# Filler products, job halves in gaps and moved gathers around the second top-k search of an attention and expert kernel

## The chip, the cores and the metric

The kernel runs on one core of a Trainium2 chip. The metric is the device time in microseconds of one execution. The core has a matrix engine (TensorE, PE in the rows), a vector engine (VectorE, DVE), an activation engine (ScalarE, ACT), a general engine (GpSimd, POOL) that also issues indirect DMAs, and a queue engine (SyncE, SP) for the other DMAs. Each runs its own instructions strictly in the order written, and they wait for one another through semaphores.

## The reference

Two sequences of 1024 tokens with 128 channels go through differential attention with 8 heads, a layer norm, an expert layer of 8 experts with top-256 tokens per expert, and a second layer norm:

```python
    x = L0_attn_X
    x = _layernorm(x + _L0_attn_ref(x, ...), axis=-1)
    x = _layernorm(x + _L0_ffn_ref(x, L0_ffn_gate_w, L0_ffn_w1, L0_ffn_w2), axis=-1)

    # the expert layer, B = 2, T = 1024, E = 8, cap = 256
        scores = jnp.einsum('BTC,CE->BTE', x, gate_w)
        probs = jax.nn.softmax(scores, axis=-1)
        top_p, top_idx = jax.lax.top_k(jnp.transpose(probs, (0, 2, 1)), cap)
        xin = jnp.take_along_axis(x[:, None, :, :], top_idx[..., None], axis=2)
        h = jax.nn.gelu(jnp.einsum('BElC,ECH->BElH', xin, w1), approximate=False)
        y = jnp.einsum('BElH,EHC->BElC', h, w2) * top_p[..., None]
        out = jnp.zeros((B, T, C), x.dtype).at[b_idx, top_idx].add(y)
```

## The kernel before, in words

Every precise matrix product is three products of float32r parts (high by high, high by low, low by high; function `three`). So each operand is rounded by one engine (the high part) and subtracted by another (the low part).

The attention takes 128 steps (16 pairs of sequence and head, 8 query tiles each). In the main loop each engine does its share of several tiles at different stages, in an order written out by hand. The expert layer of sequence 0 is prepared inside that loop: gate, search, indices, first gathers.

Behind the loop come the last outputs (`output(116)` to `output(127)`), and then what the change touches, for sequence 1 (called batch 1):

1. GpSimd computes the factors of the last outputs in groups of four (`norm_end`: a sum L632 and a power L634) once ScalarE has squared them (L814). It gathers rows for the experts of batch 0 (`gather_rows`, L651) between these groups. VectorE adds the outputs (`add_out`, L1071) with those factors.
2. TensorE transposes x1 (`x1_transposes`, L1617), VectorE copies it, TensorE multiplies it with the gate (L1628), and VectorE and ScalarE form the softmax. It is replicated, transposed again (`row_transposes`, L1642) and copied: the left half by VectorE, the right half by ScalarE (`rows_copy`, L833). ScalarE also loads the table of the Gelu here (`tick`, L962).
3. The search finds the 256th largest probability of each expert in 8 levels. In each VectorE counts (`level_count`, L1242), TensorE adds up the votes (`votes`, L1651), VectorE takes the step (`level_step`, L1258). Between them stand halves of the expert jobs of batch 0, by the table `LAST`, which names the last half done ahead of each level's vote.
4. Behind the search TensorE does small products (`limit`, `offset`, `tokens`, `counts`), VectorE the steps between them, and the indices of batch 1 come out (L1332).
5. There are 16 expert jobs (8 experts of each batch). Job q has two halves n = 2q and 2q + 1. For each job TensorE transposes the gathered rows in (`rows_in`, L1832), does `up` and, three halves later, `down`, and transposes out (`rows_out`, L1865); ScalarE rounds and does the Gelus (L881, L883); VectorE forms low parts (L1339, L1367). Jobs of batch 0 are scattered by GpSimd with an adding DMA (`scatter`, L668) into two tables in memory. Jobs of batch 1 are scaled on VectorE (L1354, L1359) and added up on TensorE with one-hot matrices (`mix`, L1876).
6. At the end SyncE loads both tables of batch 0 back (`x2_in`), VectorE adds them (`add_parts`, L1132), and TensorE turns the mixed sums of batch 1 (L1889), which VectorE adds (`add_mixed`, L1141). Then come the means (L1100), the squares on ScalarE (`ln_squares`, L768) and VectorE (`late_squares`, L1150), the variances (L1114), the powers on GpSimd (`ln_pows`, L563), and the scaling (L982, L1123) and the stores.

In the names of buffers, `xk_hi` and `xk_lo` hold expert rows here, `at_hi` and `at_lo` the results of the Gelu, `prob`, `attn` and `raw_a` are reused as storage, and `ring_a`, `ring_b`, `t_ps`, `x_ps`, `u_ps`, `o_ps` are the accumulation buffers of TensorE.

## Time and profile before

| | us |
|---|---|
| three runs, median (lowest, highest) | 909.9 (909.48, 911.5) |
| the profiled execution, its own time | 909.54 |
| span of that profile | 907.8 |
| TensorE busy / weight loads | 866.8 / 729.4 |
| ScalarE, VectorE, GpSimd busy | 748.7, 692.2, 639.6 |
| mean granted TensorE clock | 0.986 |

The span is the time from the first to the last instruction. Positions in the profile are microseconds from the span's start. A granted clock of 1.0 is TensorE at full speed and 0.50 at half. Busy times of TensorE are modelled from pipelined products, so a product's own duration is longer than the distance from its start to the start of the next.

### The profile page before, as it was taken

The numbers are of one execution on the slowest core, as the hardware profiler recorded it, in microseconds if no ns is written. First come the engines' busy times: TensorE is split into PE (matmuls) and PEld (weight loads), VectorE is DVE, ScalarE is ACT, GpSimd is POOL, SyncE is SP. The second block draws the span as 40 slices with busy tenths as digits, with TensorE's granted clock in tenths as the row PEclk, the third lists the DMA queues.
The fourth block names the chain that finished last, engine by engine and source line by source line (L and its number), as shares of the span: only waits on it lengthen the run. The fifth ranks groups of instructions, "written<-read, shape, count | busy, mean of one in ns | idle before, by whom it ended". The sixth has DMA issues, their size and how long they took to land.

```text
span 907.8 us, 14912 instructions
## 1 busy us (share of the span) xinstructions
PE 866.8 (95%) x4598; PEld 729.4 (80%) x4598; DVE 692.2 (76%) x1163; ACT 748.7 (82%) x1449; POOL 639.6 (70%) x1031
## 2 busy tenths in 40 slices
PE   6889999999999999999999999999999999877995
PEld 5668888888888888888888888888888888776984
DVE  5777777777777777777777768778898787578675
ACT  3888898888888888888889888988888889665754
POOL 1777767667776777676778866667776677769782
PEclk9999999999999999999999999999999999979898
DMA  6010010101010101001010020000000001332233
GB/s 180 13 43 16 30 31 1 59 1 58 1 59 1 47 13 36 12 19 30 1 30 1 19 58 18 15 18 16 7 24 1 19 1 44 114 82 48 50 37 99
DMA packets 41663, 30.66 MB, mean 34 GB/s; under 512 B 5825, under 2 KB 39649, under 8 KB 41585
## 3 DMA queue, kind: packets, MB, share of 16 engines
q1 hardware_dynamic: 38256, 26.44, 9.7%
q0 software_dynamic: 3328, 3.28, 2.5%
q8 instruction: 37, 0.61, 0.3%
q14 instruction: 42, 0.34, 0.1%
HBM read 20.14 MB, written 9.57 MB: 33 GB/s over the span
## 4 chain that ended last, share of the span: by engine, by line
PE 81%; POOL 6%; DVE 5%; issue 4%; ACT 2%; DMA 1%; POOLq 0%; SPq 0%; DVEq 0%; ACTq 0%
PE t_ps L1580 11%; PE ring_a L1541 6%; PE ring_a L1543 6%; PE ring_a L1542 6%; PE ring_b L1541 6%; PE ring_b L1543 6%; PE u_ps L1541 6%; PE ring_b L1542 6%; PE u_ps L1543 6%; PE u_ps L1542 6%; PE o_ps L1541 2%; PE o_ps L1542 2%; PE o_ps L1543 2%; PE x_ps L1541 2%; PE x_ps L1543 2%
## 5 line engine op out<-in xcount | busy, mean ns | idle before, releaser
L640 POOL TENSOR_TENSOR attn<-prob 128x1024 f32<-128x1024 f32 x128 | 307.4, 2402 | 173.5 <-ACT prob L799 161.8
L1056 DVE TENSOR_TENSOR at_lo<-t_ps,at_hi 128x512 fp32r<-128x512 f32 x253 | 174.1, 688 | 100.7 <-ACT at_hi L782 100.4
L1049 DVE TENSOR_REDUCE negmax<-ring_a 128x1 f32<-128x1024 f32 x128 | 156.7, 1224 | 58.6 <-PE ring_a L1543 55.7
L782 ACT ACTIVATE at_hi<-t_ps 128x512 fp32r<-128x512 f32 x253 | 151.6, 599 | 39.8 <-PE t_ps L1580 38.7
L1049 DVE TENSOR_REDUCE negmax<-ring_b 128x1 f32<-128x1024 f32 x128 | 156.2, 1220 | 2.7 <-PE ring_b L1543 1.1
L1580 PE MATMUL t_ps<-ident,attn 128*128 128x128 f32 x1012 | 152.1, 272 | 4.3 <-DVE at_lo L1056 4.1
L799 ACT ACTIVATE prob<-prob,coef 128x1024 f32<-128x1024 f32 x128 | 147.6, 1153 | 5.7 <-POOL coef L604 5.6
L1580 PEld LDWEIGHTS t_ps<-ident,attn 128*128 128x128 f32 x1012 | 124.4, 140 | 30.0 <-DVE at_lo L1056 9.4
L793 ACT ACTIVATE prob<-ring_a,negmax 128x1024 f32<-128x1024 f32 x128 | 143.1, 1118 | 4.6 <-DVE negmax L1049 4.1
L793 ACT ACTIVATE prob<-ring_b,negmax 128x1024 f32<-128x1024 f32 x128 | 142.4, 1112 | 0.6 <-DVE negmax L1049 0.5
L1541 PE MATMUL ring_b<-xt_hi,q_hi 128*128 128x512 f32 x256 | 112.0, 438 | 0.0
L1541 PE MATMUL ring_a<-xt_hi,q_hi 128*128 128x512 f32 x256 | 107.3, 419 | 0.5 <-ACT prob L793 0.4
L1543 PE MATMUL ring_a<-xt_hi,q_lo 128*128 128x512 f32 x256 | 101.3, 396 | 0.0
L1543 PE MATMUL ring_b<-xt_hi,q_lo 128*128 128x512 f32 x256 | 101.3, 396 | 0.0
L1542 PE MATMUL ring_a<-xt_lo,q_hi 128*128 128x512 f32 x256 | 100.5, 393 | 0.0
L1542 PE MATMUL ring_b<-xt_lo,q_hi 128*128 128x512 f32 x256 | 100.4, 392 | 0.0
L1541 PE MATMUL u_ps<-at_hi,xk_hi 128*128 128x512 f32 x248 | 97.8, 394 | 2.0 <-DVE u_lo L1062 2.0
L1543 PE MATMUL u_ps<-at_hi,xk_lo 128*128 128x512 f32 x248 | 97.3, 392 | 0.0
L1542 PE MATMUL u_ps<-at_lo,xk_hi 128*128 128x512 f32 x248 | 96.6, 390 | 0.0
L596 POOL TENSOR_TENSOR rs<-psum,neg_one 128x1 f32<-128x1 f32 x128 | 70.5, 551 | 14.7 <-ACT prob L793 14.5
L814 ACT ACTIVATE osq<-o_ps 128x256 f32<-128x256 f32 x117 | 44.9, 384 | 38.3 <-PE o_ps L1543 38.2
L624 POOL TENSOR_TENSOR fac<-var_o,neg_half 128x1 f32<-128x1 f32 x116 | 63.7, 549 | 16.5
(450 smaller groups left out, 1792.6 us busy)
## 6 DMA issues: line engine op xcount, KB each, us to landing
attn<-in_L_ffn_w SPq DMA_DIRECT2D x12, 256.0 KB, 3.3
ww_dram<-ww_hi SPq DMA_DIRECT2D x8, 192.0 KB, 2.5
ww_dram<-ww_lo SPq DMA_DIRECT2D x8, 192.0 KB, 2.9
ww_hi<-ww_dram SPq DMA_DIRECT2D x8, 192.0 KB, 2.4
ww_lo<-ww_dram SPq DMA_DIRECT2D x8, 192.0 KB, 2.5
wq_s<-in_L_attn_Wq SPq DMA_DIRECT2D x8, 128.0 KB, 2.7
wk_s<-in_L_attn_Wk SPq DMA_DIRECT2D x8, 128.0 KB, 3.1
xres<-in_L_attn_X SPq DMA_DIRECT2D x2, 512.0 KB, 6.3
```

The lines of the kernel that those rows point to most:

```text
L596: pool.tensor_tensor(rs2[:, par:par + 1], psum2[:, par:par + 1], neg_one[:, :], ALU.pow).then_inc(rs2_ready, 1)
L624: pool.tensor_tensor(fac[:, par:par + 1], var_o[:, par:par + 1], neg_half[:, 0:1], ALU.pow).then_inc(fac_ready, 1)
L640: pool.tensor_tensor(attn[:, t % AB, :], prob[:, t % 2, 1, :], prob[:, t % 2, 0, :], ALU.add).then_inc(attn_ready, 1)
L782: act.activation(at_hi[:, g % 2, half * GT:(half + 1) * GT, c], t_bank(t, half)[:, :].rearrange("p (k q) -> p k q", q=P), ACT.Copy).then_i ...
L793: act.activation(prob[:, par, m, :], ring[m][:, :], ACT.Exp, bias=negmax[:, par, m:m + 1], accum_out=sums).then_inc(prob_ready, 1)
L799: act.activation(prob[:, par, 1, :], prob[:, par, 1, :], ACT.Copy, scale=coef[:, par:par + 1]).then_inc(scaled_ready, 1)
L1049: dve.tensor_reduce(negmax[:, par, m:m + 1], ring[m][:, :], axis=AX.X, op=ALU.max, negate=True).then_inc(negmax_ready, 1)
L1056: dve.tensor_tensor(at_lo[:, g % 2, k, c], t_bank(t, half)[:, :].rearrange("p (k q) -> p k q", q=P), at_hi[:, g % 2, k, c].bitcast(F32), A ...
L1541: pe.matmul(dst, a_hi, b_hi, start=start, stop=False)
L1542: pe.matmul(dst, a_hi, b_lo, start=False, stop=False)
L1543: return pe.matmul(dst, a_lo, b_hi, start=False, stop=stop)
L1580: last_t = pe.transpose(t_bank(t, half)[:, k * P:(k + 1) * P], attn[:, t % AB, kk * P:(kk + 1) * P], ident[:, :])
```

## The change

In the four programs of the engines that take part:

- TensorE: 26 products whose results nobody reads (`idle_work`, 384 columns each) stand around the x1 transposes and the row transposes of batch 1. Halves of jobs 4 to 6 move between the small products behind the search. The `down` halves and the `mix` products of the last jobs stand in another order.
- GpSimd: seven of the fourteen gathers for batch 0 behind the loop stand earlier.
- ScalarE: the copy of the right half of the rows stands ahead of the Gelu's table load and `tick`. All eight squares of batch 0's norm stand ahead of the copies of the mixed sums.
- VectorE: both groups of `add_parts` stand ahead of job 15's rows, and both variances ahead of `add_mixed`.

```diff
@@ gpsimd
             norm(115)
-            for n in range(2, 7):
+            for n in range(2, 8):
                 gather_rows(n // CT, n % CT)
             norm_end(END)
-            for n in range(7, 9):
+            for n in range(8, 11):
                 gather_rows(n // CT, n % CT)
             norm_end(END + GT)
             norm_end(END + 2 * GT)
             ln_pows(1, 0)
             ln_pows(1, 1)
-            gather_rows(4, 1)
+            for n in range(11, 13):
+                gather_rows(n // CT, n % CT)
             pool.wait_ge(ln_done, 4)
             for e in range(2, E):
                 if e >= RAWS:
                     w_round(e)
                 w_lower(e)
                 if e % 2 == 1:
-                    for k in range(CT):
-                        gather_rows(5 + (e - 3) // 2, k)
+                    n = 13 + (e - 3) // 2
+                    gather_rows(n // CT, n % CT)
@@ scalar
             gate_rep(1)
+            rows_copy(1, 1)
             act.activation(tick[:, 0:1], eps_c[:, :], ACT.Gelu)
-            rows_copy(1, 1)
...
-            for c in range(GT):
+            for c in range(QT):
                 ln_squares(2, c)
             for h in range(2):
                 act.wait_ge(mixed, h + 1)
                 act.activation(sum_t[:, h * NC:(h + 1) * NC], mix_ps[h][:, :], ACT.Copy).then_inc(sum_copied, 1)
-            for c in range(GT, QT):
-                ln_squares(2, c)
@@ vector
             ffn(2 * JOBS + 1)
-            add_parts(0)
-            ln_means(2, 0)
+            for h in range(2):
+                add_parts(h)
+                ln_means(2, h)
             ffn(2 * JOBS + 3)
-            add_parts(1)
-            ln_means(2, 1)
             ln_vars(2, 0)
+            ln_vars(2, 1)
             for h in range(2):
                 add_mixed(h)
                 ln_means(3, h)
-            ln_vars(2, 1)
             late_squares()
@@ tensor
+            def idle_work(dst, count):
+
+                for _ in range(count):
+                    pe.matmul(dst, ww_hi[:, 1, 0:P], ww_hi[:, 1, 0:WWN], start=True, stop=True)
+
+            pe.wait_ge(y_added, 122)
+            idle_work(ring[0][:, 0:WWN], 4)
             x1_transposes(1, 0)
+            idle_work(ring[0][:, 0:WWN], 6)
             rows_in(0)
+            idle_work(ring[0][:, 0:WWN], 2)
             x1_transposes(1, 1)
             gate(1, range(GT))
             gate(1, range(GT, QT))
             ffn(0)
             ffn(1)
+            idle_work(quarter[2][:, 0:WWN], 6)
             row_transposes(1, 0)
             row_transposes(1, 1)
+            idle_work(quarter[2][:, 0:WWN], 8)
...
             last = LAST[LEVELS - 1]
+            down(last - 2)
             limit(1)
+            rows_in((last + 1) // 2 + 1)
+            up(last + 1)
             offset(1)
+            up(last + 2)
             tokens(1)
             counts(1, 0)
             counts(1, 1)
-            for n in range(last + 1, 2 * JOBS + 2):
+            rows_out((last + 2) // 2 - 2)
+            down(last - 1)
+            for n in range(last + 3, 2 * JOBS):
                 ffn(n)
                 if n >= 2 * E + 6 and n % 2 == 0:
                     mix(n // 2 - 3)
-            ffn(2 * JOBS + 2)
-            mix(JOBS - 2, [0])
-            ffn(2 * JOBS + 3)
-            mix(JOBS - 2, [1])
+            down(2 * JOBS - 3)
+            down(2 * JOBS - 2)
+            mix(JOBS - 3, [0])
+            rows_out(JOBS - 2)
+            down(2 * JOBS - 1)
+            mix(JOBS - 3, [1])
+            rows_out(JOBS - 1)
+            mix(JOBS - 2)
             mix(JOBS - 1)
```

What stands in a row on GpSimd behind the loop, from the last factor of the loop to the first low part of a weight (L651 is a gather, L632 and L634 are `norm_end`, L563 `ln_pows`), before:

```order
L651 DMA xg<-xg_dram,idx 128x136 x5
L632 TENSOR_TENSOR var_e<-ssq_e,es 128x4
L634 TENSOR_TENSOR fac_e<-var_e,neg_half 128x4
L651 DMA xg<-xg_dram,idx 128x136 x2
L632 TENSOR_TENSOR var_e<-ssq_e,es 128x4
L634 TENSOR_TENSOR fac_e<-var_e,neg_half 128x4
```

and in the change:

```order
L651 DMA xg<-xg_dram,idx 128x136 x6
L632 TENSOR_TENSOR var_e<-ssq_e,es 128x4
L634 TENSOR_TENSOR fac_e<-var_e,neg_half 128x4
L651 DMA xg<-xg_dram,idx 128x136 x3
L632 TENSOR_TENSOR var_e<-ssq_e,es 128x4
L634 TENSOR_TENSOR fac_e<-var_e,neg_half 128x4
```

One gather more stands ahead of the factors of outputs 116 to 119, and two more ahead of those of outputs 120 to 123.

On ScalarE, behind the softmax of the gate of batch 1 (the second row is the replication, the copy of rows reads `x_ps`, and `xk_hi` begins job 1), before:

```order
L822 ACTIVATE pr<-pr 128x64
L827 ACTIVATE prob<-pr 128x512
L962 ACT_TABLE_LOAD
L962 ACTIVATE tick<-eps_c 128x1
L833 ACTIVATE prob<-x_ps 128x512
L851 ACTIVATE xk_hi<-o_ps 128x256
L881 ACTIVATE at_hi<-ring_a 128x512
```

and in the change:

```order
L823 ACTIVATE pr<-pr 128x64
L828 ACTIVATE prob<-pr 128x512
L834 ACTIVATE prob<-x_ps 128x512
L964 ACT_TABLE_LOAD
L964 ACTIVATE tick<-eps_c 128x1
L852 ACTIVATE xk_hi<-o_ps 128x256
L882 ACTIVATE at_hi<-ring_a 128x512
```

The table load has moved behind the copy, which itself waits for the row transposes.

On VectorE at the end, from the first `add_parts` on (L1132 before, L1131 in the change; `u_hi` and `u_lo` are job 15's rows, `stat` a variance), before:

```order
L1132 SCALAR_TENSOR_TENSOR xres,rsum<-xres,attn 128x128 x4
L1100 TENSOR_SCALAR nmean<-rsum 128x4
L1354 TENSOR_TENSOR u_hi<-ring_b,prob 128x256
L1359 SCALAR_TENSOR_TENSOR u_lo<-ring_b,prob,u_hi 128x128 x2
L1132 SCALAR_TENSOR_TENSOR xres,rsum<-xres,attn 128x128 x4
L1100 TENSOR_SCALAR nmean<-rsum 128x4
L1114 TENSOR_SCALAR stat<-stat 128x4
L1141 SCALAR_TENSOR_TENSOR xres,rsum<-u_ps,xres 128x128 x4
```

and in the change:

```order
L1131 SCALAR_TENSOR_TENSOR xres,rsum<-xres,attn 128x128 x4
L1099 TENSOR_SCALAR nmean<-rsum 128x4
L1131 SCALAR_TENSOR_TENSOR xres,rsum<-xres,attn 128x128 x4
L1099 TENSOR_SCALAR nmean<-rsum 128x4
L1353 TENSOR_TENSOR u_hi<-ring_b,prob 128x256
L1358 SCALAR_TENSOR_TENSOR u_lo<-ring_b,prob,u_hi 128x128 x2
L1113 TENSOR_SCALAR stat<-stat 128x4 x2
L1140 SCALAR_TENSOR_TENSOR xres,rsum<-u_ps,xres 128x128 x4
```

Job 15's rows have moved behind the second group of adds, and both variances stand together behind them.

## Rows read from the trace of the kernel before

**Rows 1.** Busy time by stretch: us, engines busy (instructions), granted clock, DMA share, GB/s.
```profile
796.40:800.20 3.80, 1.62 (x13) 1.17 (x12) 3.19 (x19) 2.87 (x13) 1.45 (x3) 1.00 0.07 19
...
800.60:803.80 3.20, 3.20 (x16) 3.20 (x17) 2.01 (x8) 1.93 (x8) 2.21 (x3) 0.50 0.02 5
...
807.30:810.50 3.20, 0.91 (x7) 0.51 (x5) 2.74 (x6) 2.77 (x7) 3.12 (x3) 1.00 0.09 26
...
834.40:837.80 3.40, 0.99 (x6) 0.82 (x6) 3.04 (x16) 0.51 (x2) 3.04 (x2) 1.00 0.32 42
...
842.00:893.24 51.24, 49.22 (x347) 45.60 (x345) 34.64 (x73) 29.47 (x68) 37.25 (x29) 0.97 0.36 60
```

**Rows 2.** Timeline of GpSimd, 787 to 803: start, duration, what, idle before it.
```profile
787.38 1.37 POOL L651 DMA_INDIRECT xg<-xg_dram,idx  x1 [0.30 <-issue]
789.70 0.20 POOL L632 TENSOR_TENSOR var_e<-ssq_e,es 128x4 f32<-128x4 f32 x1 [0.95 <-ACT osq L814]
...
792.61 1.06 POOL L651 DMA_INDIRECT xg<-xg_dram,idx  x1 [0.30 <-issue]
794.56 0.20 POOL L632 TENSOR_TENSOR var_e<-ssq_e,es 128x4 f32<-128x4 f32 x1 [0.89 <-ACT osq L814]
...
801.77 1.04 POOL L563 TENSOR_TENSOR stat<-stat,neg_half 128x4 f32<-128x4 f32 x1 [0.81 <-DVE stat L1114]
```

**Rows 3.** Timeline of VectorE, 795 to 811.
```profile
795.91 0.35 DVE L1071 SCALAR_TENSOR_TENSOR xres<-ring_a,fac_e,xres 128x128 f32<-128x128 f32 x1 [1.93 <-POOL fac_e L634]
...
803.40 0.23 DVE L1197 TENSOR_TENSOR pr<-t_ps,stat 128x64 f32<-128x64 f32 x1 [0.68 <-PE t_ps L1628]
...
810.74 0.15 DVE L1258 TENSOR_SCALAR step<-x_ps 128x1 int32<-128x1 f32 x1
```

**Rows 4.** Timeline of ScalarE, 805 to 810.
```profile
805.86 1.28 ACT L962 ACT_TABLE_LOAD   x1
807.15 0.20 ACT L962 ACTIVATE tick<-eps_c 128x1 f32<-128x1 f32 x1
807.78 0.60 ACT L833 ACTIVATE prob<-x_ps 128x512 f32<-128x512 f32 x1 [0.43 <-PE x_ps L1642]
...
809.02 0.62 ACT L883 ACTIVATE ring_a<-ring_a 128x512 f32<-128x512 f32 x1
```

**Rows 5.** Timeline of TensorE: two output products, first rows, gate products, job 8.
```profile
795.90 0.33 PE L1542 MATMUL o_ps<-ww_lo,u_hi 128*128 128x384 f32 x1
796.07 0.34 PE L1543 MATMUL o_ps<-ww_hi,u_lo 128*128 128x384 f32 x1
...
798.93 0.41 PE L1832 MATMUL u_ps<-ident,xg 128*128 128x128 f32 x2 [1.14 <-DVE xres L1071]
...
800.15 3.21 PE L1628 MATMUL t_ps<-gate_c,prob 128*128 128x8 f32 x16
...
851.05 0.39 PE L1541 MATMUL ring_a<-xk_hi,q_hi 128*128 128x256 f32 x1 [1.07 <-DVE xk_lo L1339]
```

**Rows 6.** Timeline of VectorE, search and indices, 819 to 842.
```profile
819.62 0.69 DVE L1367 TENSOR_TENSOR at_lo<-ring_a,at_hi 128x512 fp32r<-128x512 f32 x1 [0.32 <-ACT ring_a L883]
...
840.28 0.69 DVE L1329 TENSOR_REDUCE red<-prob 128x8 f32<-128x512 bf16 x1 [1.33 <-ACT prob L837]
841.08 0.17 DVE L1332 SCALAR_TENSOR_TENSOR idx<-red,tok_c 128x8 int32<-128x8 f32 x1
```

**Rows 7.** Timeline of GpSimd: the first gather of batch 1.
```profile
842.15 1.10 POOL L651 DMA_INDIRECT prob<-xg_dram,idx  x1 [0.62 <-DVE idx L1332]
```

**Rows 8.** The chain of waits, its last 15 us: start, duration, what.
```profile
892.78 0.95 DVE xres L1132 x8
...
894.95 1.19 PE t_ps L1876 x4
...
902.24 1.12 DVE xres L1123 x4
```

**Rows 9.** Timeline of VectorE, 900 to 902.
```profile
900.84 0.29 DVE L1114 TENSOR_SCALAR stat<-stat 128x4 f32<-128x4 f32 x2
```

## The prediction

> **What bounds the kernel now.** I read the slices of the page first (TensorE is near full until the last tenth), then the busy time by stretch, then the chain of waits and the timelines behind the last attention output, since the change touches nothing earlier. Four chains follow one another there.
>
> First, from the last outputs to the second search: VectorE waits 1.93 us for GpSimd's factors, and GpSimd had itself waited 0.95 and 0.89 us for ScalarE's sums behind each of its two groups of gathers [rows 2, 3]. Then the 16 gate products take 3.21 us, because the granted clock has fallen to 0.50, the 1.2 GHz level, and VectorE waits the last 0.68 us for them [rows 1, 3, 5]. The reader should see that before the fall TensorE had done little but transposes. Second, the search: VectorE's, almost without a gap; the one that a slow TensorE causes is 0.32 us [rows 6]. Third, from the first index on, GpSimd: its first gather for batch 1 starts at 842.15 [rows 7], and 16 gathers and 12 scatters run one behind another until the last scatter has landed and is loaded back, at 892.78 [rows 8]. Fourth, the end: sums, job 15's rows, last products, norms [rows 8, 9]. TensorE is busy 49.22 of the 51.24 us of the third part, but it waited at its end for VectorE, which stood behind that load.
>
> **The change, step by step.** The sum is made against the profiled execution, 909.54 us (span 907.8 and 1.74 around it); it lies 0.36 under the median of 909.9.
>
> GpSimd's gathers. The last gather of the first group runs 787.38 to 788.75; a sixth adds an issue of 0.30 and some 1.05, so the sum behind it starts at 790.15 and not 789.70: 0.45 later. In the second group a third gather ends at 792.61 + 1.06 + 0.30 + 1.05 + 0.45 = 795.47, and the sum behind it starts at 795.5 and not 794.56: 0.94 later [rows 2]. The wait of 0.89 us that was to hide it had already been eaten by the first 0.45. VectorE waits for exactly this [rows 3], and behind its adds stand the x1 transposes, the means, ScalarE's squares and GpSimd's last power, 801.77 to 802.81 [rows 2], which moves to 803.75. Bounds: 0 if a gather overlaps the wait after all, 1.35 if neither wait hides anything. I take 0.94, since the rows give both ends.
>
> Filler products. 12 products of 384 columns stand around the x1 transposes, 6 ahead of the row transposes and 8 behind them. At full clock one costs 0.17 us (795.90 to 796.07 [rows 5]): 0.7 for the first four, which wait for VectorE's second add and end about when its fourth does, so they delay by 0 to 0.2; 1.0 for six, under a wait like the 1.14 us ahead of the first expert rows [rows 5]; 1.4 for eight, in a stretch where TensorE was busy only 0.91 of 3.20 us [rows 1]. I expect them to hold the clock. The gate products then end before GpSimd's power, and VectorE's gate step starts at 803.80 (power at 803.75) and not 803.40: +0.40 in all, the slow clock's 0.68 being repaid. The Trainium skill, TensorE: Matmul & The Clock Gate, "PE-mode transpose", says that a transpose does not count as busy for the clock; the fall behind 1.62 us of mostly transposes agrees [rows 1], and by that rule the stretch with only transposes and gate products in it remains a place where the clock may fall (the slower rival below).
>
> Row transposes and table load. ScalarE's replication ended at 805.86; with +0.40, 806.26. The two sets of row transposes behind it took until 807.75 at half clock and should be done by 807.2, so the copy of rows starts at 807.2 and not 807.78 [rows 4]. But the table load, 1.28 us plus 0.20 for the tick [rows 4], used to run under these transposes and now stands behind the copy: 807.2 + 0.60 + 1.28 + 0.20 = 809.3, then rounding and the two Gelus as before, the second at 810.05 and not 809.02. VectorE counts the first level earlier, but in its order the first job's low part stands ahead of the level's step, and it needs that Gelu, ending at 810.67. One operation of 0.60 us later the step comes at 811.28 and not 810.74 [rows 3]: +0.54. Bounds: -0.4 (no gather delay) to +0.9 (transposes no faster). The Trainium skill, ScalarE: Activation LUTs, "What ACT_TABLE_LOAD costs", puts a switch at 2.66 us, 1.38 of it a drain. Here the tick starts 1.29 us after the load; by the page the sum would be 1.38 higher.
>
> Search and indices. The search is VectorE's order, which does not change. It gets back the 0.32 us [rows 6]. Behind it TensorE now does job halves (down 9, up 12, up 13) between the small products. Each half is 6 products of 256 columns, an estimated 0.12 each by the 0.17 of 384 columns, some 0.8 us. In the stretch TensorE is idle 2.4 of 3.4 us [rows 1], in three gaps, so VectorE's small steps there don't wait for them. Their inputs are ready, since GpSimd, relieved of two gathers ahead of its last weights (an added one stands in its wait for x1), is some 2 us ahead. The stretch fills up, the clock stays, and the two products that made VectorE wait 1.33 us [rows 6] save some 0.24. The first index comes at 0.54 - 0.32 - 0.24 = -0.02.
>
> GpSimd's queue. Its first gather started 0.90 us after the index operation had ended (841.25 to 842.15), having waited 0.62 [rows 6, 7], because a scatter had only just ended. With three gathers gone from between its wait for x1 and that point it will sit and wait. I take 0.4 for that start, so -0.5 (bounds -0.7 and 0). What follows is the same 28 transfers: the load lands 0.5 earlier.
>
> TensorE in between. Job 8's first product waited 1.07 us for its rows' low parts [rows 5]; with the work ahead of it done earlier TensorE could be an estimated 1 to 2.4 us ahead from there (half the slow stretch before it is the upper end). None of it reaches the end: VectorE forms job 15's rows only after the load.
>
> The end. Before, the load released one group of adds (0.95), then job 15's rows, then the last products at 894.95 [rows 8]. Now both groups of adds stand ahead of job 15: +1.03, with TensorE, the turned sums and both later chains behind it. Repaid: GpSimd's power for the second half leaves the queue ahead of the batch 1 power. Before, the last scaling came at 902.24, behind two powers. Now it hangs on VectorE's four late squares, whose variance step is at 900.84 [rows 9], plus GpSimd's 0.2 to start and 1.1: 902.1 less the 0.13 of the step that has moved away, so the queue's gain is 0.17 to 0.27. I take +0.86 for the end; it would be -1 only if the load came ahead of job 15's rows.
>
> Sum: 0.54 - 0.32 - 0.24 - 0.5 + 0.86 = +0.34, so 909.9 us. All of it is below the 1.8 us (0.2%) that a measurement of this kernel tells from no change.
>
> **Rivals.**
> Faster, 908.1: the two queue costs don't arise. The gathers fit under GpSimd's waits (-0.94), and the load comes before TensorE reaches job 15's rows (-0.86). For it: waits of 0.95 and 0.89 stand where gathers are added. Against it: a gather with its issue is 1.35, longer than either, and GpSimd's 28 transfers leave no room to land earlier.
> Faster still, 907.1: TensorE's own chain sets the end, as its 49.22 of 51.24 busy us suggest, and up to 2.4 us reach it. Against: in the chain of waits it is the DMA and VectorE that come last [rows 8].
> Slower, 913.5: the clock falls in spite of the fillers, in the stretch from the last filler of the first dozen over the x1 transposes and the gate products to the next job half; nearly 3 us of it hold no other product. Then the 16 gate products again take 3.21, two job halves some 3.0 (12 products of twice 0.12 and their rows' transposes), the six fillers 6 x 0.33 = 2.0, and the row transposes 1.5, so the copy of rows starts at about 810.8 and not 807.2. That is +3.6 on the forecast. It decides once TensorE ends behind VectorE's replication by more than the 0.3 us it has in hand. For it: the fall with 1.62 of 3.80 us of mostly transposes.
> Slower by the drain, 911.3: if the moved table load costs 1.38 more than its row.
> It doesn't do what it says, 910.4: the fillers hold the clock first but it falls in the search or behind it as before, and 0.32 and 0.24 are not gained.
>
> **How the numbers follow.** Forecast 0.51, rival 908.1 0.17, rival 907.1 0.06, rival 913.5 0.14, drain 0.05, no effect later 0.07. The forecast's bounds, nine small terms, are about 1.4 us wide to either side: 908.5 to 911.3. The range reaches from inside the faster rivals to near the slow one: 907.6 to 912.8. Faster by over 0.2% (under 908.1): most of the two rivals and a little of the forecast, 0.24. Slower (over 911.7): 0.14, half of the drain's and a part of the forecast's tail, 0.21. Within: 0.55.
>
> **What would show it.** Granted clock 1.0 from 797 to 840. The factors for outputs 120 to 123 at 795.5 or later. The gate step released by GpSimd's power, not by TensorE. Table load behind the copy, and VectorE waiting for the first Gelu. GpSimd's first batch 1 gather released by the index, at about 841.6. VectorE idle ahead of the load while TensorE has finished job 15's rows, and the last products over 3 us behind the load. I am wrong if the first index is over 1.5 us from 841.2, if the clock falls before 807, or if the last products are not behind the load.

## The result, and the profile after

The changed kernel takes 911.64 us (median of 20 runs, 910.69 to 915.34), the kernel before 909.73 in the same series (20 runs, 908.74 to 911.76). The ratio is 1.0023, 95% interval 1.0017 to 1.0029: slower by 1.9 us, clear of no change, where "no measurable change", 909.9, had been forecast. The profiled execution took 912.22 us (span 910.3), 2.68 more than the profiled one of before, whose clock was at the better of two values: of 56 executions of the kernel before on the chip of most experiments, 27 with a mean granted clock of 0.985 or 0.986 have a median of 909.65 us, and 29 with 0.982 or 0.983 one of 911.32.

First the changed kernel's busy time by stretch, in the columns of [rows 1]: the clock is at 1.00 where [rows 1] has 0.50, but it falls in the search and again at the end. The fall in the search is not new: the last line is the kernel before, in a stretch that [rows 1] leaves out.

```profile
800.00:804.00 4.00, 3.72 (x30) 3.32 (x30) 3.33 (x17) 3.10 (x12) 1.99 (x2) 1.00 0.00 0
804.00:808.00 4.00, 3.86 (x29) 3.54 (x28) 3.34 (x12) 1.29 (x3) 2.64 (x4) 1.00 0.13 35
808.00:812.00 4.00, 1.69 (x10) 1.16 (x9) 2.88 (x8) 3.97 (x9) 3.92 (x4) 1.00 0.24 72
812.00:816.00 4.00, 3.42 (x17) 3.13 (x17) 3.83 (x10) 1.34 (x3) 3.85 (x5) 0.52 0.51 108
...
893.00:897.00 4.00, 0.88 (x4) 0.46 (x3) 3.13 (x22) 2.54 (x13) 0.39 (x1) 1.00 0.13 40
897.00:901.00 4.00, 4.00 (x15) 2.97 (x14) 0.85 (x8) 1.84 (x6) 2.05 (x4) 0.57 0.00 0
```

```profile
812.00:814.00 2.00, 1.69 (x8) 1.37 (x8) 1.89 (x8) 1.09 (x2) 1.70 (x2) 0.50 0.43 72
```

GpSimd's timeline of the changed kernel, against [rows 2, 7]. The sum for outputs 120 to 123 comes at 795.60, with no idle time left ahead of it (before: 794.56, behind 0.89). The first gather of batch 1 comes at 843.02 (before: 842.15), although GpSimd has been idle for 4.71 us.

```profile
794.54 1.02 POOL L651 DMA_INDIRECT xg<-xg_dram,idx  x1 [0.30 <-issue]
795.60 0.21 POOL L632 TENSOR_TENSOR var_e<-ssq_e,es 128x4 f32<-128x4 f32 x1
...
803.02 1.04 POOL L563 TENSOR_TENSOR stat<-stat,neg_half 128x4 f32<-128x4 f32 x1 [0.81 <-DVE stat L1113]
...
843.02 1.10 POOL L651 DMA_INDIRECT prob<-xg_dram,idx  x1 [4.71 <-DVE idx L1331]
```

VectorE's timeline, against [rows 3, 6, 8]. The gate step is now released by GpSimd, as forecast, but at 804.17 and not 803.80. The low part of the first job waits for the Gelu, and the first step comes behind it, 0.85 late. In the search a low part is waited for 0.61 us (before: 0.32). The index is 0.87 late. The load releases VectorE at 893.28, and job 15's rows stand behind both groups of adds, at 895.38 (before: 893.83).

```profile
804.17 0.23 DVE L1196 TENSOR_TENSOR pr<-t_ps,stat 128x64 f32<-128x64 f32 x1 [0.20 <-POOL stat L563]
...
810.98 0.69 DVE L1366 TENSOR_TENSOR at_lo<-ring_a,at_hi 128x512 fp32r<-128x512 f32 x1 [0.55 <-ACT ring_a L884]
811.59 0.15 DVE L1257 TENSOR_SCALAR step<-x_ps 128x1 int32<-128x1 f32 x1
...
820.76 0.69 DVE L1366 TENSOR_TENSOR at_lo<-ring_a,at_hi 128x512 fp32r<-128x512 f32 x1 [0.61 <-ACT ring_a L884]
...
841.95 0.17 DVE L1331 SCALAR_TENSOR_TENSOR idx<-red,tok_c 128x8 int32<-128x8 f32 x1
...
893.28 0.29 DVE L1131 SCALAR_TENSOR_TENSOR xres<-xres,attn 128x128 f32<-128x128 f32 x1 [2.51 <-DMA attn<-acc_dram]
...
895.38 0.42 DVE L1353 TENSOR_TENSOR u_hi<-ring_b,prob 128x256 fp32r<-128x256 f32 x1
...
904.91 2.14 DVE L1122 TENSOR_SCALAR xres<-xres,nmean,stat 128x128 f32<-128x128 f32 x8 [1.00 <-POOL stat L563]
```

ScalarE, against [rows 4]: the copy of the rows first, then the table load, 1.29 us to the tick, and the second Gelu at 810.35 instead of 809.02.

```profile
807.59 0.60 ACT L834 ACTIVATE prob<-x_ps 128x512 f32<-128x512 f32 x1 [0.98 <-PE x_ps L1640]
808.21 1.28 ACT L964 ACT_TABLE_LOAD   x1
809.50 0.20 ACT L964 ACTIVATE tick<-eps_c 128x1 f32<-128x1 f32 x1
...
810.35 0.60 ACT L884 ACTIVATE ring_a<-ring_a 128x512 f32<-128x512 f32 x1
```

TensorE at the end. In the kernel before the last products start at 894.95, behind 1.33 us of waiting, and take 0.23 from one to the next; the turn takes 0.60:

```profile
894.95 0.50 PE L1876 MATMUL t_ps<-at_lo,u_hi 128*128 128x512 f32 x1 [1.33 <-DVE u_lo L1359]
...
896.90 0.60 PE L1889 MATMUL u_ps<-ident,prob 128*128 128x128 f32 x4
```

In the changed kernel they start at 896.50, behind 3.12 us of waiting, and from the fifth on they take 0.42. The turn takes 1.05.

```profile
896.50 0.50 PE L1874 MATMUL t_ps<-at_lo,u_hi 128*128 128x512 f32 x1 [3.12 <-DVE u_lo L1358]
...
897.53 0.62 PE L1874 MATMUL x_ps<-at_lo,u_hi 128*128 128x512 f32 x1
897.95 0.63 PE L1874 MATMUL x_ps<-at_lo,u_lo 128*128 128x512 f32 x1
...
899.23 1.05 PE L1887 MATMUL u_ps<-ident,prob 128*128 128x128 f32 x4
```

So against before, in this pair of profiles: factors +1.04, gate step +0.77, first search step +0.85, first index +0.87, first gather +0.87, load +0.50, VectorE's last scaling +2.67 (902.24 to 904.91). ("Load" is VectorE's first add of the loaded tables.)

### The profile page after: what moved, and what is told of

The parts are those of the page before. It is cut to its first block, busy times and chain, and to the rows that moved or that the text cites. A ratio compares the mean times of both kernels' runs of the same rounds, so it can differ in the third digit from the quotient of the medians.

```text
span 910.3 us, 14964 instructions
## 1 busy us (share of the span) xinstructions
PE 869.8 (96%) x4624; PEld 731.3 (80%) x4624; DVE 692.8 (76%) x1163; ACT 748.0 (82%) x1449; POOL 638.9 (70%) x1031
## 4 chain that ended last, share of the span: by engine, by line
PE 79%; POOL 7%; issue 5%; DVE 5%; ACT 3%; DMA 1%; SPq 0%; POOLq 0%; DVEq 0%; ACTq 0%
PE t_ps L1578 11%; PE ring_a L1539 6%; PE ring_a L1541 6%; PE ring_a L1540 6%; PE ring_b L1539 6%; PE u_ps L1539 6%; PE ring_b L1541 6%; PE u_ps L1541 6%; PE ring_b L1540 6%; PE u_ps L1540 6%; PE o_ps L1539 2%; PE o_ps L1540 2%; PE o_ps L1541 2%; PE x_ps L1539 2%; PE x_ps L1541 1%
```

## The experiments

**Theory.** Up to the index the change costs 0.9 us. Behind the load it costs 2.2: 1.05 because both groups of adds stand ahead of job 15's rows, the rest because behind the longer wait TensorE's clock falls within the last products (0.78 in the products, 0.45 in the turn). **Rivals.** The whole loss lies ahead of the load; or the order alone counts, and the clock would have fallen anyway.

In the comparison with the kernel before, e0, e1b, e2b, e4, e5, e6, e7 and e8b ran on one chip, in two series, where the kernel before takes 910.6 to 910.7. All other runs fell on three other chips, where it takes 919.8 to 922.2. There every kernel profiled takes 26.2 to 33.8 us from the first index to the first scaled rows of batch 1 (L1353), against 18.9 to 20.7 in all others, and TensorE, not the load, ends last. Those runs say nothing on the end's wait. Ratios stand as recorded; they are not the quotients of the medians beside them.

**1. The order at the end undone** (e1, e1b), in the changed kernel:

```diff
-            for h in range(2):
-                add_parts(h)
-                ln_means(2, h)
+            add_parts(0)
+            ln_means(2, 0)
             ffn(2 * JOBS + 3)
+            add_parts(1)
+            ln_means(2, 1)
             ln_vars(2, 0)
-            ln_vars(2, 1)
...
+            ln_vars(2, 1)
             late_squares()
```

(and ScalarE's second four squares behind the copies again)

> The changed kernel with the order at the end of VectorE and ScalarE as before (one group of sums ahead of job 15's rows, the second behind); TensorE's new order of the last products stays. My theory: in the changed kernel the loaded tables release both groups of sums first (1.05 us more than one group), TensorE waits 3.12 us instead of 1.33 ahead of the last products, its clock falls at about 897.4, and the last products and the turns cost 0.78 + 0.45 more at the 1.2 GHz level. With the old order the last products start 1.05 earlier, the wait is 2.1 us, and the clock stays high: 2.1 to 2.3 us faster than the changed kernel, so 909.4 us against 911.6, the same as the kernel before (within 0.2%). Rival: only the order counts (1.05) and the clock falls anyway: 910.6. Rival: the loss lies ahead of the load, then no change, 911.6.

> The same kernel as e1_end_back again (the changed kernel with VectorE's and ScalarE's order at the end as before), since on the chip of that run TensorE lost some 10 us behind the indices in every kernel, the kernel before too, so that the load was not the last thing to come. Where the load is last (the time of the kernel before near 910 us): 2.1 us faster than the changed kernel, the same as the kernel before, 909.4. On a chip like that of the first call: no difference to the kernel before.

e1: 919.45 us, ratio 1.0000 (0.9984 to 1.0017). VectorE came to the adds at 902.56 without a wait for the load, so the order had nothing to decide. e1b: 911.15 us, ratio 1.0015 (1.0004 to 1.0026), where e0, the changed kernel on that chip, has 1.0030. By the ratios that is 1.4 us of the 2.1 expected, the two intervals overlap, and it stays slower than the kernel before. The profile shows the step itself: from the load to the last scaling it takes 9.49 us, as in the kernel before (9.46), against 11.63. VectorE and TensorE of e1b, one timeline each, with the clock full:

```profile
893.29 0.29 DVE L1133 SCALAR_TENSOR_TENSOR xres<-xres,attn 128x128 f32<-128x128 f32 x1 [2.40 <-DMA attn<-acc_dram]
```

```profile
895.47 0.50 PE L1877 MATMUL t_ps<-at_lo,u_hi 128*128 128x512 f32 x1 [1.98 <-DVE u_lo L1360]
...
897.44 0.60 PE L1890 MATMUL u_ps<-ident,prob 128*128 128x128 f32 x4
```

**2. Products in the wait at the end** (e2, e2b), between `mix(JOBS - 2)` and `mix(JOBS - 1)`:

```diff
             mix(JOBS - 2)
+            idle_work(ring[0][:, 0:WWN], 14)
             mix(JOBS - 1)
```

> The changed kernel with 14 more products whose results nobody reads (384 columns each, 2.3 us at full clock) in TensorE's wait ahead of the last eight products of the one-hot sums. My theory: the clock then stays at 1.0 through those products and the turns, their start (3.2 us behind the end of the load) doesn't move, and the time falls by 0.78 + 0.45 = 1.2 us, to 910.4 from 911.6. Rival: the clock isn't held or the half clock is hidden behind VectorE: no change, 911.6.

> The same kernel as e2_fill_before_last again (14 products without use in TensorE's wait ahead of the last eight). Where the load is last: 1.2 us faster than the changed kernel, 0.7 slower than the kernel before. On a chip like that of the first call, TensorE has no long wait there and the 14 products stand in its way: 1 to 2 us slower.

e2: 920.19 us, ratio 1.0004 (0.9988 to 1.0020). e2b: 912.81 us, ratio 1.0030 (1.0017 to 1.0043): the time did not fall. In its profile the clock did hold, in a gap of over 4 us of which the 14 products fill 2.6:

```profile
896.42 2.59 PE L1908 MATMUL ring_a<-ww_hi 128*128 128x384 f32 x14
901.08 0.50 PE L1874 MATMUL t_ps<-at_lo,u_hi 128*128 128x512 f32 x1 [2.07 <-DVE u_lo L1358]
...
903.05 0.60 PE L1887 MATMUL u_ps<-ident,prob 128*128 128x128 f32 x4
```

From job 15's rows to the last scaling it takes 8.33 us, against 9.53 in the changed kernel's first profile: 1.20, the expected size. The changed kernel itself, where its clock held at the end (e0 below), has 8.33 too. That profile, of the slowest of e2b's nine executions (915.41 us), lost elsewhere: its clock fell at about 804, its load came 51.84 us behind the first gather of batch 1 (changed kernel 50.26), and VectorE then waited 1.00 us more for the second table:

```profile
898.90 0.29 DVE L1131 SCALAR_TENSOR_TENSOR xres<-xres,attn 128x128 f32<-128x128 f32 x1 [1.00 <-DMA attn<-acc_dram]
```

The profiled execution of e7 below (915.68 us, median 913.05) has the same two lags, 51.69 and 0.90. Why such executions come is open.

**3. The order alone, in the kernel before** (e3, e3b: the first edit the other way round).

> The kernel before with only the order at the end of VectorE and ScalarE changed (both groups of sums ahead of job 15's rows, all eight squares ahead of the copies). My theory: 1.05 us for the order less 0.2 for GpSimd's queue, and 1.2 us because TensorE's wait grows from 1.33 to some 2.4 us and the clock falls: 911.8 us against 909.7 for the kernel before. If the clock survives a wait of 2.4 us: 910.6. Rival: it costs nothing since something else is last: 909.7.

> The same kernel as e3_before_end (the kernel before with both groups of sums ahead of job 15's rows and the squares together). Where the load is last: 0.95 us later from the load to the last scaling (10.4 instead of 9.46), TensorE's wait 2.4 instead of 1.33 us, and since the clock held through 1.7 to 2.1 us and fell with 3.1 us or more, it holds here: 0.9 us slower than the kernel before, ratio 1.0010. Rival: it falls and the ratio is 1.0023. On a chip like the last one: 1.000 to 1.001.

920.39 us, ratio 1.0014 (1.0000 to 1.0029), and 921.64 us, ratio 0.9993 (0.9981 to 1.0005). Both on chips where VectorE did not wait for the load. Inconclusive: the order's price in the kernel before was not measured.

**4. The gathers put back** (e4: GpSimd's part of the change undone).

> The changed kernel with GpSimd's gathers back where they were. My theory: the factors of outputs 120 to 123 come 1.04 us earlier, VectorE's adds with them, and of this at least 0.85 reaches the second search, whose first step comes at about 810.7 instead of 811.6. The first index follows by as much, GpSimd must first get through the two scatters and three gathers that stand ahead of it again, and is free only at about 841.6, so the first gather comes 0.2 to 0.4 earlier, and the load 0 to 0.4 earlier: 911.2 to 911.6 us against 911.6 for the changed kernel on the chip of the first result. Rival: the gather positions are worth their whole 0.9 us at the end: 910.7.

912.10 us, ratio 1.0019 (1.0009 to 1.0030), not told from the changed kernel. The second group takes 4.88 us from power to power (before 4.85, changed 5.33). Counted from the first gather behind the loop, the first step of the search comes at 28.89 (before 28.75, changed 29.52): the gathers cost 0.63 us there, less than the 0.85 expected. TensorE is later here, waits 1.66 us ahead of the last products, and the clock holds: 10.40 us from the load to the last scaling, 0.94 over the kernel before. That is the order by itself.

**5. The changed kernel again, and three edits at the search** (e0, e5, e6, e7, on one chip):

```diff
e5: the 26 idle_work products and their wait taken out
e6:
-            rows_copy(1, 1)
             act.activation(tick[:, 0:1], eps_c[:, :], ACT.Gelu)
+            rows_copy(1, 1)
e7:
-            idle_work(quarter[2][:, 0:WWN], 8)
+            idle_work(quarter[2][:, 0:WWN], 12)
             for lv in range(LEVELS):
                 votes(1, lv)
+                if lv == 0:
+                    idle_work(quarter[2][:, 0:WWN], 8)
```

> The changed kernel itself again, beside the next three on one chip. So far: 0.23% slower than the kernel before, where the profile showed the clock fallen ahead of the last products (1.2 us of it). If that fall is there in each execution, the ratio is again 1.0020 to 1.0028; if it comes and goes with the length of TensorE's wait (2.07 us without a fall in one run, 3.12 with it in another), the times lie in two groups about 1.2 us apart.

> The changed kernel without the 26 products without use; all else stays. Theory: the clock falls at about 800 as in the kernel before, the gate products take 3.2 instead of about 2.2 us and VectorE's gate step comes 0.5 later against the adds of the outputs; later the clock is back at the start of the search and the wait for the votes of the fourth level is 0.3 instead of 0.64 us. In all within 0.3 us of the changed kernel: the 26 products move the two slow stretches, they don't win. Rival: without them the slow stretch reaches into the row transposes and costs 1 us or more.

> The changed kernel with the Gelu's table load and tick ahead of the copy of the rows again. My theory: the load then runs from 806.6 under the row transposes, the copy ends 0.5 us later than in the changed kernel, but the first job's second Gelu comes some 0.9 earlier, so the first step of the search comes about 0.5 us earlier and the first index with it: 0.3 to 0.5 us faster than the changed kernel. Rival: VectorE waits for the later copy instead of the later Gelu, no change.

> The changed kernel with 12 instead of 8 products without use behind the row transposes, and 8 more behind the first votes, in TensorE's wait for the first job's low parts. My theory: the clock then doesn't fall at about 812, VectorE's wait for the votes of the fourth level (0.64 us, with the clock at half) shrinks to 0.1 or less, and the first index comes 0.5 us earlier relative to the first step of the search. Rival: the clock falls later on, at the next short wait, and nothing or 0.2 us is won.

e0: 912.57 us, ratio 1.0030 (1.0018 to 1.0041). Eight of its eleven times lie within 1.0 us of one another and three 2 us above, not two groups 1.2 apart, but its profile shows another course of the clock than the first. Its stretches, and ScalarE's row there:

```profile
804.00:808.00 4.00, 4.00 (x20) 3.96 (x20) 2.85 (x12) 0.89 (x2) 2.64 (x4) 0.59 0.15 35
```

```profile
808.86 0.60 ACT L834 ACTIVATE prob<-x_ps 128x512 f32<-128x512 f32 x1 [2.15 <-PE x_ps L1640]
809.48 1.28 ACT L964 ACT_TABLE_LOAD   x1
```

In spite of the 12 products the clock fell at about 803.8, behind the gate products. The twelve products of the two job halves that follow took 2.59 us instead of 1.52, the six further products 1.50 instead of 1.34 up to the transposes, which ran at full clock again but 1.3 later, and with the table load behind them the first step came 8.59 us behind the gate step, not 7.42. At the end TensorE, 2.9 us later with its work than in the first profile, then waited 1.73 us and its clock held:

```profile
898.00 0.50 PE L1874 MATMUL t_ps<-at_lo,u_hi 128*128 128x512 f32 x1 [1.73 <-DVE u_lo L1358]
...
899.98 0.60 PE L1887 MATMUL u_ps<-ident,prob 128*128 128x128 f32 x4
```

e5: 913.81 us, ratio 1.0034 (1.0020 to 1.0047). The clock falls before 800, and VectorE waits 1.26 us for the gate products: the gate step comes 9.20 us behind the power of outputs 120 to 123, with the products 8.29, in the kernel before 8.57. So the products without use earn 0.9 us at this place in the changed kernel; against the kernel before, which has none, only 0.28. The rival held: the slow stretch reached the row transposes, the first step came 31.71 us behind the first gather after the loop (e0 30.64), and the median is 1.24 us above e0's, though the two intervals overlap.

e6: 912.48 us, ratio 1.0019 (1.0010 to 1.0029). Here too the clock fell, at 804.5. The table load ran while TensorE was busy with the six products ahead of the transposes, and the first step came 7.55 us behind the gate step:

```profile
806.94 1.28 ACT L963 ACT_TABLE_LOAD   x1
808.24 0.20 ACT L963 ACTIVATE tick<-eps_c 128x1 f32<-128x1 f32 x1
809.09 0.60 ACT L834 ACTIVATE prob<-x_ps 128x512 f32<-128x512 f32 x1 [0.65 <-PE x_ps L1640]
```

So the moved load costs 1.04 us when the clock falls there (7.55 against e0's 8.59), more than the 0.5 expected. The medians of e6 and e0 are level all the same: in its profile TensorE waited 3.20 us at the end and its clock fell there. What the move costs when the clock holds is in e11b, which has the load ahead of the copy and a clock of 1.00 from 804 to 812: 6.80 us from the gate step to the first step (e15 too), against 7.42 in the changed kernel, so 0.62.

```profile
804.05 0.23 DVE L1198 TENSOR_TENSOR pr<-t_ps,stat 128x64 f32<-128x64 f32 x1 [0.20 <-POOL stat L563]
...
810.85 0.15 DVE L1259 TENSOR_SCALAR step<-x_ps 128x1 int32<-128x1 f32 x1
```

e7: 913.05 us, ratio 1.0027 (1.0015 to 1.0039). The clock stays at 1.00 from 812 to 820, and the index comes 29.97 us behind the first step, against 30.36 and 30.63 in the two profiles of the changed kernel:

```profile
812.00:816.00 4.00, 3.00 (x22) 2.55 (x21) 3.82 (x11) 2.14 (x5) 3.84 (x6) 1.00 0.52 111
816.00:820.00 4.00, 3.18 (x26) 2.82 (x24) 3.86 (x13) 2.59 (x6) 4.00 (x5) 1.00 0.78 233
```

The interval is shorter by 0.4 to 0.7 us, but I had named the wrong wait: what went is the low part's 0.61 us at 820.76, while the votes' 0.64 is at the sixth level and stays in every kernel. Nor is it shown that the added products won it: e1b, e5 and e6, without them and with a fallen clock in 812 to 816 (0.59, 0.63, 0.85), have 29.95 to 29.97 too. The slow stretch costs there as much as it makes that one Gelu late: waits of 0.40, 0.61, 0.88 and 0.89 us for it (e8b, changed, e0, e4) go with 30.12, 30.36, 30.63 and 30.64. The time did not fall measurably: TensorE waited 4.22 us at the end and its clock fell again.

**6. GpSimd's idle time used** (e8, e8b; e9 is the same edit in the kernel before):

```diff
-            for q in range(2):
+            for q in range(3):
                 scatter(q)
             gather_ready(1)
...
-            for q in range(2, E):
+            for q in range(3, E):
                 scatter(q)
```

> The changed kernel with the two scatters of job 2 issued by GpSimd ahead of its wait for the first index of batch 1 instead of behind the 16 gathers. In the changed kernel GpSimd sits idle there for 4.71 us, and two scatters with their issue take 3.75. Theory: the load at the end, which waits for the last scatter, lands 3.75 us earlier (893.3 to 889.5); then job 15's rows are released by TensorE at about 891.5 instead of by the load at 895.4, TensorE's wait shrinks from 3.12 to about 1 us and the clock stays up. 3.0 + 1.2 = 4.2 us faster than the changed kernel: 907.4 us, faster than both kernels. Rival: job 2's rows or the transfer before are not ready at 838.3, or the scatters delay the first gather, or TensorE's own chain ends as late as now: 1.2 to 2 us only, 909.6 to 910.4.

> The same kernel as e8_scatter2 again (the changed kernel with job 2's two scatters in GpSimd's wait for the first index). Where the load is last: the load lands 3.75 us earlier and the time is 4.2 us shorter than the changed kernel's, 907.4, 0.25% faster than the kernel before. On a chip like that of the first call: no difference, since there TensorE ends last.

> The kernel before with job 2's two scatters ahead of its wait for the first index, nothing else. GpSimd has only 0.62 us there, so all gathers of batch 1 start about 3.1 us later, while the last scatter ends 0.6 us earlier at most. Theory: TensorE waits 3 us more for job 8's rows and, being busy 49 of the next 51 us, ends 2 us or more later: ratio 1.001 to 1.003, slower. Rival: TensorE has slack and the load comes 0.6 earlier: 0.9995.

e8: 921.07 us, ratio 1.0011 (0.9997 to 1.0025), TensorE last. e8b: 911.25 us, ratio 1.0005 (0.9994 to 1.0017), against 1.0023 and 1.0030 for the changed kernel. Its profile is that of its fastest execution (908.24 us). The first gather is where it was, behind only 0.79 us of idling, and SyncE issues the last load 43.70 us behind it instead of 47.50: 3.8 earlier, as expected. But VectorE comes to its first add 47.69 us behind that gather instead of 50.26 and doesn't wait for the load at all; it had waited 1.78 us for TensorE's rows of job 14 (last two lines). That is the rival that TensorE's own chain ends as late as now. TensorE waits 0.52 us and its clock holds. So the gain is 2.6 us at the adds and about 2 in the time, half of what I expected, and the version is level with the kernel before, not ahead.

```profile
843.04 1.10 POOL L651 DMA_INDIRECT prob<-xg_dram,idx  x1 [0.79 <-DVE idx L1331]
...
889.75 0.42 DVE L1353 TENSOR_TENSOR u_hi<-ring_b,prob 128x256 fp32r<-128x256 f32 x1 [1.78 <-PE ring_b L1863]
...
890.73 0.28 DVE L1131 SCALAR_TENSOR_TENSOR xres<-xres,attn 128x128 f32<-128x128 f32 x1
```

e9: 921.22 us, ratio 1.0011 (1.0001 to 1.0021). The first gather starts 5.06 us behind the index instead of 1.07, and TensorE waits 0.73 and 2.27 us for its rows. The idle time that the moved gathers make is what the edit needs.

**7. The edits together** (e11: e8, e6 and e1 in one, in the changed kernel; e15: also five and two gathers in the first groups as before, three behind the powers).

> The changed kernel with three edits: job 2's scatters in GpSimd's wait for the index, the old order at the end of VectorE and ScalarE, the table load ahead of the copy of the rows again. Theory: the scatters are worth 2.6 us at the load (e8b), the order about 0.5 more (TensorE's rows of job 15, at about 891, now bind nearly as late as the load), and the table load nothing or 1.0, as TensorE's clock has it. Against the kernel before: 1.0 + 0.5 to 2 us faster, 908.0 to 909.2 where that is 910.6, a ratio of 0.997 to 0.9985. Rival: TensorE's own chain takes over and the ratio is 1.0005, as with e8b.

> The same kernel as e11_scatter2_end_table. On a chip where the kernel before takes about 910.6 and its load lands at 893: the load lands at about 890.5, TensorE reaches job 15's rows at 891, the last products start at 892.7 to 893.3 without a fall of the clock, and the last scaling at about 900.3: 907.5 to 908.7, ratio 0.9965 to 0.998 against the kernel before. On a chip like the last one again 0.998. Rival: TensorE's slow stretches take it back, ratio 0.9995 or more.

> The same as e11_scatter2_end_table with GpSimd's first two groups of gathers as short as before (five and two) and the moved ones behind the last powers: three there and four between the weights. Theory: the factors of outputs 120 to 123, the gate and the search come 0.97 us earlier; GpSimd is some 1.4 us later in front of the index and still has 3 us there, so the two scatters push the first gather by at most 0.5. 0.5 to 0.9 us faster than e11: 907.3 to 908.5, ratio 0.9965 to 0.998. Rival: the third gather behind the powers delays the weights and with them TensorE's jobs; no better than e11.

e11: 917.46 us against 919.98, ratio 0.9980 (0.9968 to 0.9993), faster than the kernel before on that chip. e11b, on another chip: 921.27 against 922.15, ratio 0.9992 (0.9980 to 1.0004), not told from no change. On the chip of e8b it was not run, so whether it beats the kernel before where the load is last stays open. e15: 920.38 us, ratio 1.0004 (0.9989 to 1.0018). Its search starts at 810.71, 1.28 earlier than e11's (0.76 of it because e11's clock fell at 804), but its first gather comes 3.43 us behind the index, against 1.07: the gathers moved back are missed where the scatters need the room. The rival's outcome, no better than e11, came by another way than the one it named.

**8. Two operations between the indices** (e13):

```diff
             indices(1, 0)
+            for w in range(2):
+                dve.reduce_sum(pst[:, 1 + w, :], sgn[1][0], AX.X)
             indices(1, 1)
```

> The changed kernel with two more sums of VectorE (0.69 us each) between the first and the second index of batch 1. In every kernel so far the first gather starts 1.07 us behind the start of the first index operation, which is also where the second index ends. If it is a latency from the first index to the gather, it stays 1.07. If the gather waits in fact for the second index or for VectorE's work there, it becomes 2.3 to 2.5 us.

921.88 us in its one run. The first index starts at 842.07, the second at 844.13, the gather at 843.15, 1.08 behind the first:

```profile
843.15 1.10 POOL L651 DMA_INDIRECT prob<-xg_dram,idx  x1 [4.72 <-DVE idx L1331]
```

It is a delay from the first index to the gather, and not a wait for the second.

Intervals read off the profiles of the chip where the load is last, in us (positions subtracted; the first two lines are the two profiles of the first comparison). A is from the first gather behind the loop to the first step of the search, B from the gate step to that step, C from it to the first index, D from VectorE's first add of the tables to its last scaling, E from job 15's rows to that scaling, F TensorE's wait ahead of the last products:

| | A | B | C | D | E | F |
|---|---|---|---|---|---|---|
| before | 28.75 | 7.34 | 30.34 | 9.46 | 8.41 | 1.33 |
| changed | 29.52 | 7.42 | 30.36 | 11.63 | 9.53 | 3.12 |
| e0, changed again | 30.64 | 8.59 | 30.63 | 10.43 | 8.33 | 1.73 |
| e1b | 29.48 | 7.44 | 29.95 | 9.49 | 8.44 | 1.98 |
| e2b | 30.62 | 8.59 | 30.68 | 11.52 | 8.33 | 2.07, behind the 14 products |
| e4 | 28.89 | 7.43 | 30.64 | 10.40 | 8.31 | 1.66 |
| e5 | 31.71 | 8.78 | 29.97 | 11.97 | 9.88 | 3.23 |
| e6 | 29.57 | 7.55 | 29.97 | 11.95 | 9.86 | 3.20 |
| e7 | 30.63 | 8.61 | 29.97 | 13.48 | 10.39 | 4.22 |
| e8b | 29.44 | 7.43 | 30.12 | 10.41 | 8.32 | 0.52 |

## Why the prediction was wrong, point by point

The forecast was no measurable change; the kernel became slower by 1.9 us. The two steps that failed are the first index, forecast at -0.02 and measured at +0.87, and the end, forecast at +0.86 and measured at +2.17. None of the signs under "I am wrong if" came in the first profile: its index lies 0.75 us from 841.2, its clock holds to 812, and the last products are behind the load.

**GpSimd's gathers:** right in mechanism and size, 1.04 us against 0.94, and 0.96 counted from the first gather behind the loop. Two more gathers with their issues are 2.7 us; GpSimd's two waits took up the rest.

**Filler products:** partly right. The gate step is released by GpSimd's power, but it is 0.77 late and not 0.40: 0.2 because the first four products delay the transposes by the upper end of my 0 to 0.2 (VectorE waits 0.74 us for them, before 0.54), 0.1 from the gathers, the rest between the power and the step. "I expect them to hold the clock" is wrong as a certainty: it held in the changed kernel's first profile, in e1b, e4 and e8b, and fell between 802.9 and 804.5 in e0, e2b, e6 and e7. The rival at 913.5 is thus real, but its price at the first step is 1.2 us, not 3.6: the fall comes behind the gate products or in the last of them, and the transposes run at full clock again. Slow are the twelve products of the two job halves and the six behind them.

**Table load:** right where the clock holds, too small where it falls. The first step came 0.85 late, not 0.54, but 0.77 of it was there at the gate step, and the 0.08 added behind that is near the forecast's 0.14. It is a difference of two terms: the moved load costs 0.62 (e11b, e15), and TensorE's full clock gives 0.54 back. With a fallen clock the load costs 1.04 (e0 against e6). The load itself is as before, 1.29 us to the tick. The Trainium skill, ScalarE: Activation LUTs, "What ACT_TABLE_LOAD costs", would have a drain of 1.38 on top; no run here shows it at this place.

**Search and indices:** failed. I let the search get back 0.32 us and the small products 0.24, on a clock at 1.0 up to 840. It fell at 812, as in the kernel before, behind a stretch in which TensorE was busy 1.69 of 4 us; the last of the products without use end at 809.0, and TensorE then waits for the first job's low parts. From the first step to the index it took what it took before, 30.36 against 30.34: the low part's wait grew from 0.32 to 0.61 instead of going, and only the wait ahead of the index shrank by 0.2, as forecast, with the clock at 1.00 there. In e1b, e5, e6 and e7 the 0.4 is there. My rival "it doesn't do what it says" describes this step. The forecast's index at -0.02 became +0.87: 0.37 of the miss was there at the gate step, and 0.58 arose behind the first step.

**GpSimd's queue:** this step failed in its mechanism. I took 0.4 us for the start of the first gather when GpSimd sits idle. It is 0.90 behind the index operation's end in every kernel where GpSimd was free, with 0.62, 4.71 or 6.19 us of idling before it (e13 fixes the cause to the first index). What I took for a queue was never one. That 0.37 us was given back all the same, close to my 0.5, is luck: it came between gather and load, where nothing was forecast, and what gave it is not shown. In the profiles with 12 scatters behind the gathers that distance is 50.14 to 51.84 us.

**The end:** right in its mechanism, short of one term. The order costs 0.94 to 0.97 (e4, e0 against before, undone in e1b), as the forecast's 0.86 says. The term that I left out: TensorE's wait ahead of the last products grows from 1.33 to 3.12 us (1.05 by the order, 0.50 by the later load, 0.25 because TensorE itself is done earlier), its clock falls within them, and they and the turn cost 1.2 more. The prediction had "the last products over 3 us behind the load" among its own signs, and did not price what TensorE does meanwhile. This fall is in the first profile of the changed kernel, in e5, e6 and e7, which waited 3.12 to 4.22 us, and not in those that waited 0.52 to 2.07. The same kernel gives its size: 9.53 us from job 15's rows to the last scaling with the fall, 8.33 without (e0), and e2b, with the wait filled, has 8.33. In e5, e6 and e7 it is 1.5 to 2.1 us.

Added up, +0.34 became +2.67 in the first pair of profiles: 0.87 at the index (forecast -0.02), less 0.37 up to the load (forecast -0.5), plus 2.17 behind it (forecast +0.86). Between the medians it is 1.9. That not each execution has each fall would explain this, and that single steps repair so little in the medians (1.0015 to 1.0034 in seven kernels, each to 0.1%), but how often each fall comes was not measured. No run takes back all the steps that cost, so their sum is read from profiles and not shown in the times.

## What to carry to other kernels

Price a longer wait of TensorE with the clock too: here what stood behind the four longest waits ran in part or whole at 1.2 GHz, and nothing came after these last products to hide it. An operation that ran under another engine's slow work, as the table load did, is free only as long as it stays there: moved, it cost 0.62 us even with the other engine fast. And read the kernel before over the whole stretch that a change is to speed up: the fall in the search stood in its profile. When a reordering makes an engine idle, look for work behind its wait that could fill the gap, since the idle time itself shortens nothing.

## What the runs showed of the hardware

- An indirect gather on GpSimd starts 0.90 us behind the end of the operation that makes its index (1.07 to 1.08 behind its start, in the changed kernel, before, e0, e1b, e4 and e13), with 0.62 to 6.19 us of idling before it.
- The same program had its slow stretches at different places in two executions: 0.59 at 804 to 808 in e0, 1.00 there in the changed kernel's first profile. With the 12 filler products four of seven profiles on that chip have a fall right behind the gate products or, in e7, in the last of them (the second eight take 1.16 us, in the changed kernel 1.03).
- On three chips the kernel before took 919.8 to 922.2 us instead of 909.7 to 910.7. From the first index to batch 1's first scaled rows the profiles there show 26.2 to 33.8 us instead of 18.9 to 20.7, with waits between 855 and 877 for many of which they name no releaser. TensorE, ScalarE and VectorE stood there together while GpSimd's 16 gathers took as long as elsewhere (21.0 to 21.8 us from first to last; 20.9 to 21.7). The cause is open.
